# Two heads share one 32-column tile of the values' products, and a batch's sums fill 256 columns of PSUM instead of 512

## What is computed

```
q = split_heads(Q @ Wq);  k = split_heads(K @ Wk);  v = split_heads(V @ Wv)   # 16 heads x 128 x 8
scores = einsum('bhqd,bhkd->bhqk', q, k) / sqrt(8)       # layer 1: also a mask, and causal
probs = softmax(scores, axis=-1)
out = einsum('bhqk,bhkd->bhqd', probs, v)                # "the values' products"
out = out.transpose(0, 2, 1, 3).reshape(B, S, 128)       # heads side by side again
x = x + out @ Wo
```

## Time and profile before

| | us |
|---|---|
| median of 3 runs | 421.1 |
| lowest, highest | 419.34, 424.3 |
| span of the profiled execution | 422.1 |
| attention 0, from the first scores to the last step | about 39 to 124 |
| experts | about 124 to 280 |
| attention 1 | about 280 to 377 |
| TensorE busy | 352.5 (84%) |
| VectorE busy | 279.8 (66%) |
| ScalarE busy | 220.8 (52%) |
| GpSimd busy | 124.8 (30%) |

### The profile page before, as it was taken

How to read it: one execution, slowest core, us unless ns; L and a number is a source line. 1 busy time by engine, 2 the same in 40 slices (tenths; PEclk the granted TensorE clock), 3 DMA queues, 4 the chain that set the end, 5 groups by cost and what they waited for, 6 DMA issues and landing times. The chain is left out here.

```text
span 422.1 us, 10432 instructions
## 1 busy us (share of the span) xinstructions
PE 352.5 (84%) x3418; PEld 255.7 (61%) x3418; DVE 279.8 (66%) x871; ACT 220.8 (52%) x426; POOL 124.8 (30%) x231
## 2 busy tenths in 40 slices
PE   1584779999978999999999999789899899746563
PEld 0353568777754777667667767557677677633342
DVE  6674768988836553662542443586778989458994
ACT  2143346776766735444344344137455575647884
POOL 6325041242532102101001001135445554521332
PEclk9977669999998999999999999859999999887999
DMA  6555964443144003620170100103444431000011
GB/s 198 141 152 111 246 163 122 143 142 121 53 143 136 2 2 62 134 54 2 37 209 17 37 0 0 37 4 117 105 117 113 116 115 59 1 2 0 26 33 44
DMA packets 54100, 34.98 MB, mean 83 GB/s; under 512 B 38744, under 2 KB 46256, under 8 KB 54064
## 3 DMA queue, kind: packets, MB, share of 16 engines
q1 hardware_dynamic: 44032, 31.43, 27.6%
q10 hardware_dynamic: 10032, 3.08, 3.0%
HBM read 24.60 MB, written 9.44 MB: 81 GB/s over the span
## 5 line engine op out<-in xcount | busy, mean ns | idle before, releaser
L1064 ACT ACTIVATE probs<-ps_e 128x512 f32<-128x512 f32 x128 | 76.1, 596 | 55.5 <-PE ps_e L899 52.1
L975 DVE TENSOR_REDUCE neg<-ps_s 128x4 f32<-128x512 f32 x128 | 86.0, 685 | 26.2 <-PE ps_s L882 24.3
L1326 DVE SCALAR_TENSOR_TENSOR x_all<-ps_ym,c_g,x_all 128x128 f32 (+1 forms) x128 | 36.0, 343 | 63.2 <-PE ps_ym L1421 63.1
L1421 PEld LDWEIGHTS ps_ym<-w,hid 128*128 128x128 f32 x512 | 60.8, 192 | 9.2 <-issue 6.7
L882 PE MATMUL ps_s<-k_rows,q_rows 96*128 96x128 bf16 x512 | 55.0, 236 | 10.8 <-DVE neg L975 4.0
L1421 PE MATMUL ps_ym<-w,hid 128*128 128x128 f32 x512 | 62.2, 276 | 0.0
L1411 PE MATMUL ps_h<-tok_t,w 128*128 (+1 forms) x128 | 61.5, 603 | 0.0
L1528 ACT ACTIVATE hid<-ps_h,b 128x512 f32<-128x512 f32 x64 | 43.2, 684 | 34.8 <-PE ps_h L1411 33.4
L882 PEld LDWEIGHTS ps_s<-k_rows,q_rows 96*128 96x128 bf16 x512 | 40.8, 106 | 25.3 <-issue 11.3
L899 PE MATMUL ps_e<-q_rows,k_rows 128*128 128x128 bf16 x512 | 52.0, 228 | 2.8 <-DMA q_rows<-neg_t 2.0
L899 PEld LDWEIGHTS ps_e<-q_rows,k_rows 128*128 128x128 bf16 x512 | 37.0, 102 | 6.5 <-DMA q_rows<-neg_t 2.7
(11 more groups left out here) (206 smaller groups left out, 548.8 us busy)
## 6 DMA issues: line engine op xcount, KB each, us to landing
k_rows<-k_dram SPq DMA_DIRECT2D x32, 144.0 KB
q_rows<-q_dram SPq DMA_DIRECT2D x32, 144.0 KB
k_rows<-k_dram SPq DMA_DIRECT2D x16, 288.0 KB
q_rows<-q_dram SPq DMA_DIRECT2D x16, 288.0 KB
k_dram<-parts SPq DMA_DIRECT2D x35, 128.0 KB, 2.4
w<-in_w SPq DMA_DIRECT2D x16, 128.0 KB, 2.7
q_dram<-parts SPq DMA_DIRECT2D x15, 128.0 KB, 2.2
q_dram<-parts ACTq DMA_DIRECT2D x9, 128.0 KB, 3.0
```

The lines of the kernel that those rows point to most:

```text
L975: dve.tensor_reduce(neg[:, s, q * HQ:(q + 1) * HQ], ps_s[:, q % 2, :].rearrange("p (h k) -> p h k", h=HQ), AX_X, ALU.max, negate=True).the ...
L1064: act.activation(probs[:, s, q, :], ps_e[:, q % 2, :], ACT.Exp, scale=SCALE).then_inc(exp_done, 1)
L1326: dve.scalar_tensor_tensor(out=batch_of(x_all, g * G + j), in0=ps_y[:, e % 2, j * D:(j + 1) * D], scalar=c_g[:, j, e:e + 1], in1=batch_of( ...
L1421: last = pe.matmul(ps_y[:, e % 2, j * D:(j + 1) * D], hid[:, (e % 2) * M + m, j * P:(j + 1) * P], w2[:, e, m, :], start=(m == 0), stop=(m ...
```

## The change

The sums of two heads are put into one 32-column tile: the even head's 9 results in rows 0 to 8 of the tile, the odd head's in rows 16 to 24. For this the quarters take other heads (`head(q, j)`): quarter 0 has heads 0, 2, 4, 6; quarter 1 has 1, 3, 5, 7; quarter 2 has 8, 10, 12, 14; quarter 3 the odd ones to 15. `v_aug` holds for each pair 64 columns: the even head's stationary operand is the first 32 (its values in columns 0 to 8, zeros behind), the odd head's the last 32 (zeros, then its values in 16 to 24). The even head's matmul starts the accumulation, the odd head's, one quarter later, adds to it. So the number of matmuls of V and their shapes stay, and their results fill 256 columns. `copy_sums` copies 256 columns instead of 512, and `turn_back` turns two blocks of 128 instead of four. The maxima of a quarter are written with a step of two; `fill` writes the same 128 values of a batch in another pattern; the ones are set by two memsets at the start of each attention instead of one.

```diff
+        def head(q, j):
+            return (q // 2) * 2 * HQ + 2 * j + q % 2
...
-        v_aug = sb("v_aug", [P, 2, H, VW], F32)
-        o_t = sb("o_t", [P, 2, W], F32)
+        v_aug = sb("v_aug", [P, 2, H // 2, 4, HW], F32)
+        o_t = sb("o_t", [P, 2, OW], F32)
...
                 for j in range(HQ):
-                    h = q * HQ + j
+                    h = head(q, j)
...
                 for j in range(HQ):
-                    last = pe.matmul(ps_v[VW * j:VW * (j + 1), q * P:(q + 1) * P], v_aug[:, s, q * HQ + j, :],
-                                     probs[:, s, q, j * P:(j + 1) * P], start=True, stop=True)
+                    pair = v_aug[:, s, head(q, j) // 2].rearrange("p a c -> p (a c)")
+                    last = pe.matmul(ps_v[VW * j:VW * (j + 1), (q // 2) * P:(q // 2 + 1) * P],
+                                     pair[:, (q % 2) * VW:(q % 2 + 1) * VW], probs[:, s, q, j * P:(j + 1) * P],
+                                     start=(q % 2 == 0), stop=(q % 2 == 1))
...
-                for q in range(NQ):
-                    last = pe.transpose(ps_o[:, q * P:(q + 1) * P], o_t[:, s, q * P:(q + 1) * P], ident[:])
+                for n in range(NQ // 2):
+                    last = pe.transpose(ps_o[:, n * P:(n + 1) * P], o_t[:, s, n * P:(n + 1) * P], ident[:])
...
-                dve.tensor_reduce(neg[:, s, q * HQ:(q + 1) * HQ], ps_s[:, q % 2, :].rearrange("p (h k) -> p h k", h=HQ),
+                dve.tensor_reduce(neg[:, s, head(q, 0):head(q, HQ - 1) + 1:2], ps_s[:, q % 2, :].rearrange("p (h k) -> p h k", h=HQ),
...
-                heads = ps_o[:].rearrange("p (h c) -> p h c", h=H)
+                heads = ps_o[:, 0:OW].rearrange("p (h c) -> p h c", h=H)
...
-                act.activation(o_t[:, s, :], ps_v[:], ACT.Copy).then_inc(ot_ready, 1)
+                act.activation(o_t[:, s, :], ps_v[:, 0:OW], ACT.Copy).then_inc(ot_ready, 1)
...
-                pool.tensor_tensor(v_aug[:, s, :, 0:DK],
+                pool.tensor_tensor(v_aug[:, s, :, 0:4:3, 0:DK],
```

More of the change, by code:

```diff
@@ L740, in attention @@
         VW = 32
+        HW = VW // 2
+        OW = NQ // 2 * P
+        def head(q, j):
+            return (q // 2) * 2 * HQ + 2 * j + q % 2
         selected = (0, 1, 2) if layer == 1 else ()
@@ L1118, in _ @@
             pool.wait_ge(cleared, 2)
-            pool.memset(v_aug[:, :, :, DK:DK + 1], 1.0).then_inc(cleared, 1)
-            pool.wait_ge(cleared, 3)
+            for s in range(2):
+                pool.memset(v_aug[:, s, :, 0:4:3, DK:DK + 1], 1.0).then_inc(cleared, 1)
+            pool.wait_ge(cleared, 4)
             def fill(b, s):
                 wait(pool, pv_done, (b - 1) * NQ)
-                pool.tensor_tensor(v_aug[:, s, :, 0:DK],
-                                   c["v"][:, layer, bass.ds(b, 1), :].rearrange("p b (h d) -> p (b h) d", h=H),
-                                   c["zero"][:].rearrange("p (h d) -> p h d", h=H), ALU.add)\
+                pool.tensor_tensor(v_aug[:, s, :, 0:4:3, 0:DK],
+                                   c["v"][:, layer, bass.ds(b, 1), :].rearrange("p b (g n d) -> p (b g) n d", n=2, d=DK),
+                                   c["zero"][:].rearrange("p (g n d) -> p g n d", n=2, d=DK), ALU.add)\
                     .then_inc(vaug_ready, 1)
@@ L1154, in add_bias @@
                                    ALU.add).then_inc(cleared, 1)
-                pool.wait_ge(cleared, 4)
+                pool.wait_ge(cleared, 5)
             def leave_queries():
```

## The result

| | before | after |
|---|---|---|
| median, same chip, 20 runs each | 422.73 us | 419.90 us |
| lowest, highest | 419.34, 428.01 | 417.59, 423.24 |
| ratio, 95% interval | | 0.9941, 0.9921 to 0.9960 |
| span of the profiled execution | 422.1 | 417.9 |

The change takes 2.5 us off (0.0059 x 422.7; 1.7 to 3.3 by the interval). Two of the 20 runs of the kernel before (427.74 and 428.01) fell in a slower state, which the ratio leaves out. A second comparison gave 0.9926 (0.9895 to 0.9957), 3.1 us. The forecast was 414.7 us and 6.4 us less. Of the 5.2 us between 419.9 and the forecast, 1.6 are the base (the median of 3 runs was 421.1, that of 20 is 422.7), the other 3.6 are the change itself: it brings 2.5 to 3.1, not 6.4.

A forecast was written before the change was run, and what follows sets the result against it. TensorE and VectorE, both near their limit in a closed loop, were taken to bound the attentions, with loads also limiting attention 1. Attention 0's 3.3 and attention 1's 3.1 made 6.4 us, 421.1 - 6.4 = 414.7 us; range 410.5 to 419.

The forecast's parts named there:

- the copy: ScalarE's copy of the sums: 256 columns about 0.375 us, 0.205 less, counting only where P waits for `oo_t`.
- TB: TensorE's transposes of the sums: four hold it 0.43 us, two cost 0.215, all on the stretch from S2 to M3.
- term c: V's 16 matmuls, second head added onto the first's columns: taken as 0, bounded above by +0.71 us a step.
- rival 3: Accumulating breaks the tiles' overlap: V grows by up to 0.71 us in all 32 steps, total 428; chance 0.05.
- Attention 0, steps 6 to 13: Steps 6, 7, 10, 11 give 0; steps 8, 9, 12, 13 give 0.3 us each, 1.2 in all.
- the full steps: Steps with pieces of statistics, where VectorE reaches M3 without idle time: 0 gain; in attention 0 steps 6, 7, 10, 11.
- Attention 0, steps 3 to 5: P doesn't wait there, so only the transposes count: 3 x 0.215 = 0.65 us.
- The last steps: Both cuts count at 0.42 us a step: attention 0's steps 14 to 16 give 1.26, attention 1's last three 1.04.
- Attention 1, the steps 2 and 3: Part of steps 1 to 6, where loads limit and two steps together shrink by 0.365 us: 1.1 in all.
- Attention 1, steps 4 to 13: Steps to 6 shrink 0.365 us per two; 7, 8, 11, 12 give 0; 9, 10, 13 give 1.0 together.
- Rival 1: Transfers take the gain: laying takes 2.41 us in every step, loads get no earlier; 417.2 to 418.8 us; chance 0.22.
- the open steps of attention 0: Steps 8, 9, 12, 13, where VectorE idles 0.48 to 0.68 us before M3; 0.3 each, between 0.18 and 0.42.

The follow-up runs named there:

- pairs_only: The changed kernel with four transposes and the 512-column copy given back, only the tile sharing left; against the kernel before 1.0014 (0.9975 to 1.0053).
- after_again: The changed kernel measured once more, with a second trace; 0.9926 (0.9895 to 0.9957) of the kernel before.
- before_aside: The kernel before with lays of `neg_t` from the fifth batch on written to an unread tile, so E0 doesn't wait; 1.0015 of the kernel before.
- after_aside: The changed kernel with lays of `neg_t` from the fifth batch on written to an unread tile, so E0 doesn't wait; 0.9889 of the kernel before.
- after_layact: The changed kernel with the lay of `neg_t` issued by ScalarE, not SyncE, in both attentions; 1.0241 (1.0199 to 1.0284) of the kernel before.
- copy_cut: The changed kernel with four transposes a step again, the 256-column copy kept; 0.9918 (0.9879 to 0.9958) of the kernel before.

## Why the prediction was wrong

The direction and the prices of the two cuts were right: the copy at 0.36 (0.375 predicted), TB at 0.22 (0.215), V unchanged (term c, and rival 3 is excluded by pairs_only). Term c had argued from two records for each matmul of V; they don't show by themselves that one adds onto the other, and it is the run that settles it. What failed is what the sum assumed to be late next: it took the gain of the steps at both ends of attention 0 in full, and it took steps 2 and 3 of attention 1 as any others. "Measured" is the difference of after and of after_again from the one trace of before, in the table.

1. *Attention 0, steps 6 to 13: right in size and place, but not for the reason given.* 1.2 predicted, 1.24 and 1.05 measured. From V to V the gain seems to lie in the full steps (6, 7, 10, 11: 18.53 before, 17.67 and 17.54 after). That is an effect of where the step is cut. Measured from the end of one M3 to the end of the next, which is VectorE's own step, the full ones last 18.48 before and 18.57 and 18.71 after (predicted: no gain), and 8, 9, 12 and 13 last 18.36 before and 16.94 and 16.97 after, 0.35 a step (predicted: 0.3). But the 0.3 came from a guess between two bounds of the lay, and with the lay aside this gain is the same (18.23 to 16.92). In after, steps 9 and 13 gained 0.40, nearly all of the 0.42; in step 12 M3 follows VectorE's work without idle time, so there VectorE is what is next. The lay was late once in these four, at the end of step 9 (issued 92.45, S0 at 94.42, E0 at 94.94, where E0 otherwise stands 0.22 behind S0); the next step is a full one and took 4.74 by M3, 4.73 before, so this delay cost nothing. At the ends of steps 8 and 12 E0 started 2.27 us after the lay's issue, on time. The part of the timeline that shows how VectorE reached M3 in steps 12 and 13 of the changed kernel:

```profile
107.32 1.51 DVE L984 TENSOR_REDUCE neg<-ps_s 128x4 f32<-128x512 f32 x2
...
112.30 0.69 DVE L984 TENSOR_REDUCE neg<-ps_s 128x4 f32<-128x512 f32 x1 [0.28 <-PE ps_s L889]
```

2. *Attention 0, steps 3 to 5: 0.65 predicted, -0.25 and +0.13 measured (0.34 between the means of four traces each).* Here lies the failed step. I let the lay limit only steps 8, 9, 12 and 13, where it didn't, and counted the transposes in full in 3 to 5. Steps 3 and 5 did gain (4.52 and 4.50 us to 4.18 and 4.24). Step 4 did not (4.53 to 5.38): a long issue of a load stands ahead of the lay, and E0 waited 1.02 us. With the lay aside the three steps last 12.40 in two traces: 1.10 less than before_aside's, more than predicted, since there the copy counts too. P stood 0.31 us behind E2 in before_aside's step 4 and 0.22 in after_aside's; so P did wait a little where I had read "without a wait" from the earlier trace rows.
3. *The last steps: in attention 0, 0.84 predicted for 14 and 15 and 0.51 measured; in attention 1, 0.84 predicted and 0.59 measured at the full clock (9.18 to 8.59).* Step 14 hits the lay's own 2.13 us (issued 114.46, used 116.59); with the lay aside both pairs of steps gain 0.85, as summed. Here the sum had no term for the lay at all.
4. *Attention 1, the steps 2 and 3: some 0.4 of the 1.1 for steps 1 to 6; -0.97 and +0.64 measured.* The sum had overlooked ScalarE's stores, which wait for VectorE's split of the queries: TensorE came early to a wait that hadn't moved, and in some executions paid with the half clock, 1.5 us. With the stores later, the change gains 0.04 in these steps.
5. *Attention 1, steps 4 to 13: about 1.55 predicted, 1.7 measured in both traces.* The six kernels of the table without a cut in attention 1 spread from 55.2 to 57.6 there (mean 56.1), the eight with one or both from 54.1 to 55.8 (mean 54.8), so 1.3 on the mean. Right in size.

Rival 1 (transfers take the gain, 3.9 down to 2.3 us) had the size of what was measured, but only in part its mechanism. It let the lay take the gain of the open steps of attention 0 (0.18 left in each; they gave 0.35) and left 0.3 in steps 3 to 5 (0.34 by the means), but counted the last steps in full; in attention 1 it isn't the transfers but the stores. I gave it 0.22 with the argument that P's waits outweigh the loads' in attention 1, which is true and says nothing on the lay in attention 0. The pairs show where it went: the change is worth 2.5 to 3.1 us as it is, 4.0 with late stores, 5.3 without the lay. Open is the exact split: the intervals of the pairs overlap, and in the medians the two edits together didn't add, though in the steps they did. Open is what makes the issue of a load in step 4 take 0.9 us in one trace and 1.6 in another. Open is also why the half clock comes in some executions only. With the change in attention 1 and the stores in place, the four traces in which step 2 took 4.95 us had it in step 3, and of four with a longer step 2 (5.17, 6.05, 6.13, 6.32) only after_layact's had it. That points to the load that holds step 2 or doesn't; it wasn't tested by itself.

## What to carry to other kernels

A cut in a closed loop is worth what is late next, and that has to be asked in each kind of step, the irregular ones above all: here the sum of the regular steps came out within 0.15 us, and the errors that could be placed lay in the first steps, the last ones, and two that did something else on the side. Here the lay of `neg_t` took 2.1 to 2.6 us from issue to use, however short the step around it; such a wait can cost nothing that a time shows today and come up when the loop gets shorter (before_aside: nothing to be told from zero; after_aside: about half of what the change could bring). Before cutting, list such fixed points with their slack; moving one (the stores, one number in one line) brought another 2 us, almost as much as the change. And measure a step on the engine that closes the loop: cut at V, the same traces put the gain in the wrong steps.

## What the runs showed of the hardware

- Issuing the 12 KB lay holds the issuing engine for 0.70 to 0.77 us on SyncE and 0.73 on ScalarE, but the store of query parts only 0.38 on ScalarE. A load's issue mostly takes 0.76 to 0.79, but one in step 4 of attention 0 took 0.89 to 1.64 in 16 of the 17 traces with four loads a batch. The price of an issue has to be read for the very transfer and place.
- fp32 matmuls that add a second operand onto the same columns of a 32-column tile, one quarter after the first, run at the same pace as into fresh ones: 1.01 us for V either way.
- After two waits of 0.99 and 0.66 us the granted clock fell to the lower level for 3.2 us, in a stretch in which TensorE was otherwise busy; after one wait of 0.88, or one of 1.01 a step earlier, it stayed at the full one. copy_cut had the same two waits (0.99 and 0.66) and kept the full clock (1.00), and the kernel before fell behind waits of 0.67 and 0.88 at the end of attention 1 where pairs_only, with the same two waits, did not. So these waits alone don't decide it.
